# A fused decoder's first stage: batch 1 split at the start, its linear product behind batch 0's, key stores and loads in another order

## The chip, the cores and the metric

The kernel runs on one core of a Trainium2 chip. The core has five engines that run their own instruction streams and wait for each other on semaphores: TensorE (PE), VectorE (DVE), ScalarE (ACT), GpSimd (POOL) and SyncE (SP), which here only waits and issues transfers. Transfers (DMA) run on 16 engines of their own. The metric is the device time of the whole kernel in microseconds, the median of some runs.

## The reference, cut to what matters

A decoder of two layers on `x` (16 batches x 112 tokens x 1024), float32. Each step adds its result to its input and normalises the sum.

```python
x = layernorm(x + x @ (W0 * blockmask).T + bias)            # L0 "attention": a block-masked linear layer
x = layernorm(x + xattn(x, ctx, ctx, mask))                 # 32 heads of 32, 8 shared key/value heads, 375 context rows
x = layernorm(x + gated_slot_ffn(x))                        # routing to 8 of 256 slots, a learned gate
x = layernorm(x + L1_attention(x))                          # causal, over the batch
x = layernorm(x + xattn(x, ctx, ctx, mask))
x = layernorm(x + routed_low_rank_ffn(x))
```

The first line and the cross attention of the first layer are what the change touches. `blockmask` switches 32 x 32 blocks of the 1024 x 1024 weight off; the kernel itself sums the mask over the blocks, masks the weights and splits them.

## The kernel before, in words

The program has three stages: `token_stage` for layer 0 (lines, cross attention and slot layer, batch by batch), `self_attention`, and `token_stage` for layer 1. A float32 product is made of three products of rounded parts (`split_passes`): high by high, high by low, low by high. So each operand is first copied to a high part (`x_hi`, by ScalarE) and the rest is taken as the low part (`x_lo`, by GpSimd or VectorE).

In `token_stage` every engine runs the same loop over turns t (`turns`), from t = -3 in layer 0. In turn t the attention of batch t is computed in 32 steps n (one head each: score, masked minimum, exponential, transposition, weighted values), and beside it the linear layer of batch t + 2, the queries of batch t + 1 and the end of batches t - 1 and t - 2. `on(lag)` says whether batch t + lag exists. The order on each engine is exactly the order in which the code issues; nothing moves it later. The work of an engine waits where it stands, and all that is behind it on the engine waits too.

The lead-in (turns -3 to -1 of layer 0):
- SyncE loads `xt` (the transposed x of batch 0), eight chunks of the block mask and eight of the weights through six buffers (`load_weights`), the bias, `xb` (x of batch 0 by rows), `xt` of batch 1, `craw` (transposed context) and, when the weights are done, the raw weights of the slot layer (`load_update`).
- VectorE reduces the mask chunks (L1064), masks the weights (L1079) and takes their low parts (L1072), then negates the attention mask `nmask` (L1084).
- TensorE makes batch 0's linear product while the weights come (`first_linear`), VectorE adds it to `xb` and normalises it (`linear`, L455) to `xnew`; TensorE transposes `xnew` to queries (L464), ScalarE and VectorE take the parts (`qT_hi`, `qT_lo`).
- Batch 1 follows in turn -1: `xt` split at the end of turn -2 (L771, L438), 48 products (L473), the addition and the normalisation.
- The query parts and the parts of the context (`c_hi`, `c_lo`, scaled) are stored to HBM (`query_parts`, `ctx_parts`) and read back in the layout of the heads: `krep` and `qrep`, halves 0 and 1, four loads each (L256, L273). A score (L482) needs its half of both (semaphore `ld_kq`).

The steps the prediction speaks of are L771 (`x_hi`), L438 (`x_lo`), L762 (`qT_hi`), L1051 (`qT_lo`), L749 (`probs`, the exponential) and L482 (scores). ScalarE's wait for `xt` reads:

```python
if first and on(3) and n == 25:
    if on(2):
        act.wait_ge(lin_ok, 2 * (t + 3))
    act.wait_ge(ld_xt, w.next(ld_xt, 16))
    nc.scalar.copy(x_hi[:], xt[:]).then_inc(x_hi_ok, 1)
```

## Time and profile before

| | us |
|---|---|
| median of 3 runs | 3253.34 (3253.17 to 3255.41) |
| the profiled execution | 3256.68 |
| its span, first to last instruction | 3254.9 |

The page's first two sections: busy time and share of each engine, and the span in 40 slices of 81 us, each digit a busy share in tenths. PEclk is the granted clock of TensorE in tenths of full speed.

```profile
span 3254.9 us, 67042 instructions
...
PE 3086.3 (95%) x25912; PEld 2573.2 (79%) x25912; DVE 1804.2 (55%) x4632; ACT 1340.0 (41%) x3692; POOL 872.4 (27%) x751
...
PE   5999999986899999999999999999999699999997
PEld 3888888874788888888878888888887588888886
DVE  6788888885434432444253323333243488888885
ACT  2777877783211111111111111111111487877773
POOL 2222222212423432243225332443233001111110
PEclk8999999996899999999999999999999799999998
DMA  9777787763112311231144111221124555556651
```

TensorE is busy for 95% of the span. The first slice holds the lead-in, with TensorE at 5 tenths.

### The profile page before, as it was taken

To read this page: it belongs to the slowest core of one execution; us is meant where nothing else is said; L and a number is where in the kernel's file an instruction comes from. 1 tells how busy PE (TensorE), PEld (TensorE's weight loads), DVE (VectorE), ACT (ScalarE), POOL (GpSimd) and SP (SyncE) were. 2 spreads that over 40 slices of the span, in tenths; PEclk is the share of its full clock that TensorE was granted. 3 is DMA by queue.
4 is the path that set the end of the run, shared out by engine and by line. 5 is a ranking of instruction groups with operands and counts; after the bars stand their busy time and mean duration, and the time that the engine had idled before them with its cause. 6 is when DMAs were issued, how large, how long until landed. Compare 5 with 4: busy or idle time off the path is not lost. (4 is left out here: it accounts for less than half of the span.)

```text
span 3254.9 us, 67042 instructions
## 1 busy us (share of the span) xinstructions
PE 3086.3 (95%) x25912; PEld 2573.2 (79%) x25912; DVE 1804.2 (55%) x4632; ACT 1340.0 (41%) x3692; POOL 872.4 (27%) x751
## 2 busy tenths in 40 slices
PE   5999999986899999999999999999999699999997
PEld 3888888874788888888878888888887588888886
DVE  6788888885434432444253323333243488888885
ACT  2777877783211111111111111111111487877773
POOL 2222222212423432243225332443233001111110
PEclk8999999996899999999999999999999799999998
DMA  9777787763112311231144111221124555556651
GB/s 279 191 188 190 191 202 189 183 149 99 53 58 79 91 53 58 72 91 59 51 164 143 53 59 61 83 79 52 52 72 162 157 146 152 153 151 153 152 147 36
DMA packets 226622, 386.73 MB, mean 119 GB/s; under 512 B 55953, under 2 KB 177137, under 8 KB 225794
## 3 DMA queue, kind: packets, MB, share of 16 engines
q1 hardware_dynamic: 222848, 380.25, 42.2%
q8 instruction: 207, 3.39, 0.5%
q10 hardware_dynamic: 3458, 2.20, 0.2%
q14 instruction: 109, 0.89, 0.1%
HBM read 291.46 MB, written 90.91 MB: 117 GB/s over the span
## 5 line engine op out<-in xcount | busy, mean ns | idle before, releaser
L749 ACT ACTIVATE L_probs<-L_masked,L_least 112x375 f32<-112x375 f32 x1024 | 627.9, 615 | 79.1 <-DVE L_least L878 74.9
L878 DVE CUSTOM_DVE_ANT_0 L_masked<-L_scores,L_nmask 112x375 f32<-112x375 f32 x1024 | 553.1, 544 | 172.3 <-PE L_scores L482 135.3
L1445 PE MATMUL sa_banks<-both_hi,sa_w_hi 128*128 128x480 f32 (+2 forms) x1536 | 559.7, 364 | 2.0 <-DVE both_lo L1706 2.0
L1445 PE MATMUL sa_banks<-both_lo,sa_w_hi 128*128 128x480 f32 (+2 forms) x1536 | 550.2, 358 | 0.0
L1445 PE MATMUL sa_banks<-both_hi,sa_w_lo 128*128 128x480 f32 (+2 forms) x1536 | 549.5, 358 | 0.0
L487 PEld LDWEIGHTS L_turned<-ident_sb,L_probs 112*125 112x125 f32 x3072 | 456.2, 189 | 106.0 <-issue 48.1
L487 PE MATMUL L_turned<-ident_sb,L_probs 112*125 112x112 f32 x3072 | 525.2, 280 | 6.5 <-ACT L_probsT L744 3.3
L482 PE MATMUL L_scores<-L_krep,L_qrep 128*112 128x376 f32 x1024 | 417.2, 408 | 8.1 <-DMA L_qrep<-query_parts 6.2
L744 ACT COPY L_probsT<-L_turned 125x336 f32<-125x336 f32 x768 | 337.4, 439 | 175.2 <-PE L_turned L487 168.1
L1747 DVE TENSOR_TENSOR sa_acc<-sa_acc,sa_banks 128x512 f32<-128x512 f32 x224 | 154.1, 688 | 416.5 <-PE sa_banks L1504 416.5
L1504 PE MATMUL sa_banks<-sa_p_hi,sa_o_hi 128*128 128x512 f32 x896 | 365.2, 408 | 0.0
L1504 PE MATMUL sa_banks<-sa_p_lo,sa_o_hi 128*128 128x512 f32 x896 | 355.1, 396 | 0.0
L1504 PE MATMUL sa_banks<-sa_p_hi,sa_o_lo 128*128 128x512 f32 x896 | 355.0, 396 | 0.0
L1445 PEld LDWEIGHTS sa_banks<-both_hi,sa_w_hi 128*128 128x128 f32 x1536 | 288.9, 188 | 34.5 <-issue 6.8
L1713 DVE SCALAR_TENSOR_TENSOR sa_sm<-sa_banks,sa_causal 128x224 f32<-128x224 f32 x64 | 25.1, 392 | 511.2 <-PE sa_banks L1466 511.2
L1445 PEld LDWEIGHTS sa_banks<-both_hi,sa_w_lo 128*128 128x128 f32 x1536 | 288.7, 188 | 23.3
L1445 PEld LDWEIGHTS sa_banks<-both_lo,sa_w_hi 128*128 128x128 f32 x1536 | 289.1, 188 | 21.6
L1614 ACT CAST sa_o_hi<-sa_banks 128x512 fp32r<-128x512 f32 x112 | 66.0, 589 | 508.0 <-PE sa_banks L1487 506.4
L384 POOL TENSOR_TENSOR L_attn<-L_attn,L_xcur 112x512 f32<-112x512 f32 x64 | 82.5, 1288 | 584.2 <-DVEq L891 584.2
L1388 POOL TENSOR_TENSOR sa_w_lo<-sa_raw,sa_w_hi 128x1024 fp32r<-128x1024 f32 x96 | 229.9, 2394 | 14.5 <-issue 1.6
L1386 POOL CAST sa_p_hi<-sa_raw 128x1024 fp32r<-128x1024 f32 x64 | 66.5, 1039 | 564.3 <-PE sa_banks L1504 554.5
L1504 PEld LDWEIGHTS sa_banks<-sa_p_hi,sa_o_hi 128*128 128x128 f32 x896 | 169.0, 189 | 47.9 <-issue 0.4
(289 smaller groups left out, 5054.2 us busy)
## 6 DMA issues: line engine op xcount, KB each, us to landing
L_qrep<-query_parts SPq DMA_DIRECT2D x256, 224.0 KB, 6.2
sa_raw<-in_wqkvU_dram SPq DMA_DIRECT2D x96, 512.0 KB, 3.5
L_krep<-ctx_parts SPq DMA_DIRECT2D x256, 188.0 KB, 4.3
sa_raw<-in_wprojU_dram SPq DMA_DIRECT2D x64, 512.0 KB, 3.5
query_parts<-L_qT_hi SPq DMA_DIRECT2D x64, 224.0 KB, 8.3
query_parts<-L_qT_lo SPq DMA_DIRECT2D x64, 224.0 KB, 9.4
L_xcur<-x SPq DMA_DIRECT2D x32, 448.0 KB, 5.0
L_val<-in_ctx_dram SPq DMA_DIRECT2D x64, 187.5 KB
```

Source lines behind the costliest of these rows:

```text
L384: p.tensor_tensor(attn[0:S, cols], attn[0:S, cols], xcur[0:S, cols], ALU.add).then_inc(sum_ok, 1)
L482: pe.matmul(scores[0:S, (NH * t + n) % 3, 0:TP], qrep[:, gq, r, gi, :], krep[:, 4 * gq + gi, :], start=True, stop=True).then_inc(score_ok, 1)
L487: mm = pe.transpose(turned[0:TC, m % 2, S * j:S * j + S], probs[0:S, m % 4, TC * j:TC * j + TC], ident[0:S, 0:S])
L744: nc.scalar.copy(probsT[:, m % 8, :, :], turned[0:TC, m % 2, 0:TJ * S].rearrange("p (j s) -> p j s", s=S)).then_inc(copied_s, 1)
L749: nc.scalar.activation(probs[0:S, e % 4, :], masked[0:S, e % 4, :], ACT.Exp, bias=least[0:S, e:e + 1], scale=-1.0, accum_out=rsum[0:S, e:e ...
L878: v.tensor_tensor_reduce(out=masked[0:S, n % 4, :], in0=scores[0:S, (NH * t + n) % 3, 0:T], in1=nmask[0:S, :], scale=1.0, scalar=HUGE, op0 ...
L1386: nc.gpsimd.tensor_copy(hi, src)
L1388: done = nc.gpsimd.tensor_tensor(lo, src, hi.bitcast(F32), ALU.subtract)
L1445: mm = pe.matmul(feat[u % 2][i][:, 0:t.stop - t.start], a[:, u % 2, k, :], b[:, k, t], start=(n == 0), stop=(n == 3 * KT - 1))
L1504: mm = pe.matmul(out, a[:, j, c % 2, :], b[:, j, 512 * h:512 * h + 512], start=(i == 0), stop=(i == 3 * QPG - 1))
L1614: nc.scalar.copy(o_hi[:, :, c % 2, :].rearrange("p j (b t) -> p j b t", b=4), mixed).then_inc(o_hi_ok, 1)
L1747: v.tensor_tensor(acc[:, c, cols], acc[:, c, cols], ring[:, b, :], ALU.add).then_inc(ring_free[b], 1)
```

## The change

All of it is in the lead-in of the first stage; line numbers of the changed kernel are about 28 to 46 higher.

- `xT[1]` is loaded at the very beginning, in front of `xT[0]`, into `oT`, and split in turn -3 into `tT_hi` and `tT_lo` (buffers that are free until turn 1). The linear product of batch 1 reads these.
- The first 16 of the 24 products of batch 1's first half stand right behind batch 0's product on TensorE (`HEADSTART`), behind VectorE's reading of the bank.
- `nmask` is negated as VectorE's first work, and waits for the small loads. The bias addition of batch 0 waits until the weights are done (`chunk_done`).
- The parts of batch 0's context are taken in turn -2 and stored (`store_keys`) behind `load_update`. In turn -1 SyncE waits for `x_free`, loads `xb`, stores the queries of batch 0, then `x1`, and loads `krep` half 0, `qrep` half 0, `krep` half 1, `qrep` half 1, both halves of `val`, `craw` of batch 1 and `xt` of batch 2, in this order.
- ScalarE's high part of batch 2's `xt` stands at step 8 of turn -1.

ScalarE before, from its last work on the weights to the first exponentials of turn 0. `L_ra` is a table load, `L_c_hi` the context's high part:

```order
L820 DMA L_ra<-in_valuesT_dram 128x256 x2
L771 CAST L_x_hi<-L_xt 128x896 [waits L0_ld_xt,L0_lin_ok]
L762 CAST L_qT_hi<-L_wide 128x448 [waits L0_turn] x2
L766 ACTIVATE L_c_hi<-L_craw 128x2x375 [waits L0_ld_c]
L771 CAST L_x_hi<-L_xt 128x896 [waits L0_ld_xt,L0_lin_ok]
L762 CAST L_qT_hi<-L_wide 128x448 [waits L0_qT_free,L0_turn]
L749 ACTIVATE L_probs,L_rsum<-L_masked,L_least 112x375 [waits L0_least] x3
L762 CAST L_qT_hi<-L_wide 128x448 [waits L0_turn]
L749 ACTIVATE L_probs,L_rsum<-L_masked,L_least 112x375 [waits L0_least]
L766 ACTIVATE L_c_hi<-L_craw 128x2x375 [waits L0_ld_c]
```

And in the changed kernel, the same stretch:

```order
L861 DMA L_ra<-in_valuesT_dram 128x256 x2
L803 ACTIVATE L_c_hi<-L_craw 128x2x375 [waits L0_ld_c]
L799 CAST L_qT_hi<-L_wide 128x448 [waits L0_turn] x2
L810 CAST L_x_hi<-L_xt 128x896 [waits L0_ld_xt,L0_lin_ok]
L799 CAST L_qT_hi<-L_wide 128x448 [waits L0_qT_free,L0_turn]
L786 ACTIVATE L_probs,L_rsum<-L_masked,L_least 112x375 [waits L0_least] x3
L799 CAST L_qT_hi<-L_wide 128x448 [waits L0_turn]
L786 ACTIVATE L_probs,L_rsum<-L_masked,L_least 112x375 [waits L0_least]
L803 ACTIVATE L_c_hi<-L_craw 128x2x375 [waits L0_ld_c]
```

The context's part has moved ahead of the queries, the split of `xt` for batch 1 is gone from here (it is done at the start), and the split for batch 2 (L810) stands where the one of L771 stood, in front of batch 1's query part and the exponentials.

SyncE before, from the load of `xb` for batch 1 (L298) to half 0 of `krep` for batch 0:

```order
L298 DMA L_xb<-in_x_dram 112x1024
L302 DMA L_xt<-in_xT_dram 128x896 [waits L0_xt_free]
L266 DMA query_parts<-L_qT_hi 128x448 [waits L0_q_lo]
L266 DMA query_parts<-L_qT_lo 128x448
L266 DMA query_parts<-L_qT_hi 128x448 [waits L0_q_lo]
L266 DMA query_parts<-L_qT_lo 128x448
L321 DMA ctx_parts<-L_c_hi 128x376 [waits L0_c_lo_ok]
L321 DMA ctx_parts<-L_c_hi 128x376
L321 DMA ctx_parts<-L_c_lo 128x376 x2
L323 DMA L_craw<-in_ctxT_dram 128x750
L256 DMA L_krep<-ctx_parts 32x4x376 [waits L0_c_stored]
L256 DMA L_krep<-ctx_parts 32x4x376 x3
```

In the changed kernel, from the queries' last stores to `xt` of batch 2:

```order
L266 DMA query_parts<-L_qT_hi 128x448 [waits L0_q_lo]
L266 DMA query_parts<-L_qT_lo 128x448
L330 DMA x<-L_xnew 112x1024
L256 DMA L_krep<-ctx_parts 32x4x376 [waits L0_c_stored]
L256 DMA L_krep<-ctx_parts 32x4x376 x3
L273 DMA L_qrep<-query_parts 32x4x448 [waits L0_q_stored]
L273 DMA L_qrep<-query_parts 32x4x448 x3
L256 DMA L_krep<-ctx_parts 32x4x376 x4
L273 DMA L_qrep<-query_parts 32x4x448 x4
L260 DMA L_val<-in_ctx_dram 125x3x128 x2
L372 DMA L_craw<-in_ctxT_dram 128x750
L374 DMA L_xt<-in_xT_dram 128x896 [waits L0_xt_free]
```

The load of `xt` for batch 2 stood in front of the query stores; it now stands behind all loads of batch 0's keys, queries and values. The key stores (L280) are ahead of this piece.

The diff:

```diff
@@ -273,6 +273,12 @@
 
+            def store_keys(w, nb):
+                sp.wait_ge(c_lo_ok, w.next(c_lo_ok))
+                for part, src in ((0, c_hi), (1, c_lo)):
+                    for h in range(2):
+                        sp.dma_start(ks[nb, part, h], src[:, h, :].bitcast(F32)).then_inc(c_stored, 16)
+
@@ -287,6 +293,7 @@
                 sp.wait_ge(chunk_done, 2 * KT)
+                sp.wait_ge(split_x, 2)
@@ -294,10 +301,14 @@
                     load_weights()
+                if first and t == -1:
+                    sp.wait_ge(x_free, w.next(x_free))
...
                     sp.dma_start(xb[0:S, :], io["x"][t + 2]).then_inc(ld_x, 16)
-                if first and on(3):
-                    if on(2):
+                if first and on(3) and t not in (-2, -1):
+                    if t == -3:
+                        sp.dma_start(oT[:], io["xT"][1]).then_inc(ld_xt, 16)
+                    else:
@@ -307,22 +318,25 @@
                         sp.wait_ge(k_free[1], w.next(k_free[1]))
-                    if first or t:
+                    if t:
                         load_keys(t, 1)
-                    load_queries(t, 1)
+                    if not first or t:
+                        load_queries(t, 1)
...
                     store_queries(w, t + 1, 1)
-                if first and on(1):
-                    sp.wait_ge(c_lo_ok, w.next(c_lo_ok))
-                    for part, src in ((0, c_hi), (1, c_lo)):
-                        for h in range(2):
-                            sp.dma_start(ks[t + 1, part, h], src[:, h, :].bitcast(F32)).then_inc(c_stored, 16)
-                if first and on(2):
+                if first and t == -1:
+                    sp.dma_start(io["x1"][0], xnew[0:S, :]).then_inc(x1_stored, 16)
+                    sp.wait_ge(c_stored, w.next(c_stored, 64))
+                    load_keys(0, 0)
+                if first and on(1) and t >= 0:
+                    store_keys(w, t + 1)
+                if first and on(2) and t != -1:
...
                     load_update()
+                    store_keys(w, 0)
@@ -330,7 +344,7 @@
                         sp.wait_ge(v_free[1], w.next(v_free[1]))
-                    if first or t:
+                    if t:
@@ -340,30 +354,40 @@
                 if on(1):
-                    if first:
+                    if first and t >= 0:
...
                         sp.wait_ge(k_free[0], w.next(k_free[0]))
-                    if first or t >= 0:
+                    if t >= 0:
...
                     load_queries(t + 1, 0)
-                    if not first and t == -1:
+                    if t == -1:
                         load_keys(0, 1)
+                    if first and t == -1:
+                        load_queries(0, 1)
+                        load_values(0, 0)
+                        load_values(0, 1)
+                        sp.dma_start(craw[:], io["ctxT"][1]).then_inc(ld_c, 16)
+                        sp.wait_ge(xt_free, w.next(xt_free))
+                        sp.dma_start(xt[:], io["xT"][2]).then_inc(ld_xt, 16)
...
                     sp.dma_start(io["rows"][t - 2][:, D:D + BOT + 2], z_row[0:S, :]).then_inc(z_stored, 16)
-                if first and on(2):
+                if first and on(2) and t > -2:
...
                         sp.wait_ge(v_free[0], w.next(v_free[0]))
-                    load_values(t + 1, 0 if first or t >= 0 else 1)
+                    if t >= 0:
+                        load_values(t + 1, 0)
+                    elif not first:
+                        load_values(0, 1)
@@ -413,6 +437,7 @@
                         pool.wait_ge(ld_bias, 16)
+                        pool.wait_ge(chunk_done, 2 * KT)
@@ -431,12 +456,15 @@
                     residual(w, 0)
-                if first and on(3):
+                if first and on(3) and t != -2:
...
                     pool.drain().then_inc(xt_free, 1)
+                    if t == -3:
+                        pool.wait_ge(x_hi_ok, w.next(x_hi_ok))
+                        p.tensor_tensor(tT_lo[:], oT[:], tT_hi[:].bitcast(F32), ALU.subtract).then_inc(split_x, 1)
@@ -580,25 +608,34 @@
 
+            HEADSTART = 16
+
...
                     pe.wait_ge(lin_read, w.next(lin_read))
+                left = (tT_hi, tT_lo) if t == -1 else (x_hi, x_lo)
...
                         first_linear(w)
+                        pe.wait_ge(split_x, w.next(split_x))
+                        pe.wait_ge(lin_read, 1)
+                        products(spare[0:S, :], (tT_hi, tT_lo), (w0_hi, w0_lo), slice(0, 512), KT, 0, HEADSTART)
...
                         pe.wait_ge(ra_ok, t - 1)
-                    pe.wait_ge(split_x, w.next(split_x))
+                    if t >= 0:
+                        pe.wait_ge(split_x, w.next(split_x))
...
                     i, j = dealt(LIN[h], n)
+                    if t == -1 and h == 0:
+                        i = max(i, HEADSTART)
                     if i < j:
-                        mm = products(bank[0:S, :], (x_hi, x_lo), (w0_hi, w0_lo), slice(512 * h, 512 * h + 512), KT, i, j)
+                        mm = products(bank[0:S, :], left, (w0_hi, w0_lo), slice(512 * h, 512 * h + 512), KT, i, j)
@@ -761,14 +798,18 @@
                                        wide[:, 0, 0:4 * S].rearrange("p (k s) -> p k s", s=S)).then_inc(q_hi_ok, 1)
-                if first and on(1) and n == 4:
+                if first and ((t, n) == (-2, 24) or on(1) and t >= 0 and n == 4):
...
                     nc.scalar.mul(c_hi[:, :, 0:T], craw[:], -float(HD) ** -0.5).then_inc(c_hi_ok, 1)
-                if first and on(3) and n == 25:
-                    if on(2):
+                if first and on(3) and t != -2 and n == (8 if t == -1 else 25):
+                    if t >= 0:
                         act.wait_ge(lin_ok, 2 * (t + 3))
-                    act.wait_ge(ld_xt, w.next(ld_xt, 16))
+                    if t == -1:
+                        act.wait_ge(lin_ok, 2)
+                    act.wait_ge(ld_xt, w.next(ld_xt, 32 if t == -3 else 16))
                     nc.scalar.copy(x_hi[:], xt[:]).then_inc(x_hi_ok, 1)
+                    if t == -3:
+                        nc.scalar.copy(tT_hi[:], oT[:]).then_inc(x_hi_ok, 1)
@@ -1044,7 +1085,7 @@
 
-            def queries(w, n, on):
+            def queries(t, w, n, on):
@@ -1053,12 +1094,17 @@
                             dve.sem_inc(x_free, 1)
-                if first and on(1) and n == 7:
-                    dve.wait_ge(c_hi_ok, w.next(c_hi_ok))
-                    v.scalar_tensor_tensor(out=c_lo[:, :, 0:T], in0=craw[:], scalar=-float(HD) ** -0.5,
-                                           in1=c_hi[:, :, 0:T].bitcast(F32), op0=ALU.mult, op1=ALU.subtract).then_inc(c_lo_ok, 1)
+                if first and on(1) and t >= 0 and n == 7:
+                    low_keys(w)
+
+            def low_keys(w):
+                dve.wait_ge(c_hi_ok, w.next(c_hi_ok))
+                v.scalar_tensor_tensor(out=c_lo[:, :, 0:T], in0=craw[:], scalar=-float(HD) ** -0.5,
+                                       in1=c_hi[:, :, 0:T].bitcast(F32), op0=ALU.mult, op1=ALU.subtract).then_inc(c_lo_ok, 1)
             def masked_weights():
+                dve.wait_ge(small_in, 16 * len(small))
+                v.tensor_scalar(nmask[0:S, :], nmask[0:S, :], -1.0, None, ALU.mult)
@@ -1080,8 +1126,6 @@
                 low(KT - 1)
-                dve.wait_ge(small_in, 16 * len(small))
-                v.tensor_scalar(nmask[0:S, :], nmask[0:S, :], -1.0, None, ALU.mult)
@@ -1105,7 +1149,9 @@
                     tokens(t, w, n, on)
-                    queries(w, n, on)
+                    queries(t, w, n, on)
+                    if first and (t, n) == (-2, 26):
+                        low_keys(w)
...
                             linear(w, n, on)
```

## Rows read from the trace of the kernel before

**Rows 1.** Waits of TensorE, 66 to 200 us: us in total, times, longest.
```profile
PE L_scores L482 <- DMA L_qrep<-query_parts: 1.9, 1, 1.9
```

**Rows 2.** Timeline near the first scores: start, length (us), engine line op [idle before <-releaser].
```profile
60.30 0.94 ACT L771 CAST L_x_hi<-L_xt 128x896 fp32r<-128x896 f32 x1 [10.83 <-PE L_wide L473]
...
66.98 1.28 PE L482 MATMUL L_scores<-L_krep,L_qrep 128*112 128x376 f32 x3 [1.85 <-DMA L_qrep<-query_parts]
...
68.15 0.62 DVE L1051 TENSOR_TENSOR L_qT_lo<-L_wide,L_qT_hi 128x448 fp32r<-128x448 f32 x1
...
68.82 1.01 PE L464 MATMUL L_wide<-ident_sb,L_xnew 112*128 112x112 f32 x4 [0.56 <-DVE L_qT_lo L1051]
```

**Rows 3.** Timeline, SyncE's queue, key stores and key loads.
```profile
51.77 1.26 SPq L321 DMA_DIRECT2D ctx_parts<-L_c_lo  x2
...
56.99 1.76 SPq L256 DMA_DIRECT2D L_krep<-ctx_parts  x4
```

**Rows 4.** Windows: busy PE, PEld, DVE, ACT, POOL, PEclk, DMA share, GB/s.
```profile
10.00:12.00 2.00, 0.00 (x0) 0.00 (x0) 1.96 (x2) 0.00 (x0) 0.00 (x0) 1.00 1.02 410
...
62.00:64.00 2.00, 0.00 (x0) 0.00 (x0) 0.94 (x2) 0.00 (x0) 0.79 (x2) 0.96 1.05 217
```

**Rows 5.** Timeline of VectorE, lead-in.
```profile
6.39 1.22 DVE L1064 TENSOR_REDUCE L_brow<-L_attn 128x32 f32<-128x1024 int32 x1 [5.26 <-DMA L_attn<-in_bmaskT_dram]
...
15.97 1.22 DVE L1064 TENSOR_REDUCE L_brow<-L_row 128x32 f32<-128x1024 int32 x1
...
35.04 1.22 DVE L1072 TENSOR_TENSOR L_w_lo<-L_xnew,L_w_hi 128x1024 fp32r<-128x1024 f32 x1
36.23 2.24 DVE L1072 TENSOR_TENSOR L_w_lo<-L_xcur,L_w_hi 128x1024 fp32r<-128x1024 f32 x1
38.40 1.44 DVE L1084 TENSOR_SCALAR L_nmask<-L_nmask 112x375 f32<-112x375 f32 x1
...
43.94 0.81 DVE L455 TENSOR_SCALAR L_xnew<-L_xb,L_mv,L_rstd 112x1024 f32<-112x1024 f32 x1 [1.07 <-POOL L_rstd L379]
```

**Rows 6.** Tile nmask: its load (ns min/median/max, first to last start) and its landing.
```profile
L812 ACTq DMA_DIRECT2D L_nmask<-in_mask_dram x1: 452/452/452, 1.7 to 1.7; - x1
...
DMA to landing us min/median/max: 6.7/6.7/6.7
```

**Rows 7.** Timeline of GpSimd, the bias addition and a low half.
```profile
33.61 6.01 POOL L390 TENSOR_TENSOR L_xb<-L_xb,L_bias 112x512 f32<-112x512 f32 x2 [25.64 <-DMA L_xb<-in_x_dram]
...
51.01 2.54 POOL L390 TENSOR_TENSOR L_xb<-L_xb,L_bias 112x512 f32<-112x512 f32 x2 [4.04 <-DMA L_xb<-in_x_dram]
...
64.15 2.07 POOL L438 TENSOR_TENSOR L_x_lo<-L_xt,L_x_hi 128x896 fp32r<-128x896 f32 x1 [0.99 <-DVE L_xnew L455]
```

**Rows 8.** Timeline, first and last of 48 products; VectorE's normalised rows behind them.
```profile
47.85 0.75 PE L473 MATMUL L_spare<-L_w_hi,L_x_hi 128*112 128x512 f32 x1
...
59.86 0.40 PE L473 MATMUL L_wide<-L_w_hi,L_x_lo 128*112 128x512 f32 x1
...
63.19 0.81 DVE L455 TENSOR_SCALAR L_xnew<-L_xb,L_mv,L_rstd 112x1024 f32<-112x1024 f32 x1 [1.06 <-POOL L_rstd L379]
```

**Rows 9.** DMA issues, 50 to 64 us: count, KB each, us from issue to landing.
```profile
L_qrep<-query_parts SPq DMA_DIRECT2D x4, 224.0 KB, 6.0
L_krep<-ctx_parts SPq DMA_DIRECT2D x4, 188.0 KB, 3.7
x<-L_xnew SPq DMA_DIRECT2D x1, 448.0 KB, 4.2
...
query_parts<-L_qT_lo SPq DMA_DIRECT2D x1, 224.0 KB, 4.7
```

**Rows 10.** DMA issues of the whole page, section 6.
```profile
L_val<-in_ctx_dram SPq DMA_DIRECT2D x64, 187.5 KB
```

**Rows 11.** Timeline of ScalarE, batch 1's query copy.
```profile
65.17 0.53 ACT L762 CAST L_qT_hi<-L_wide 128x448 fp32r<-128x448 f32 x1 [3.93 <-PE L_wide L464]
```

**Rows 12.** DMA issues, 64 to 80 us, the load of xt.
```profile
L_xt<-in_xT_dram SPq DMA_DIRECT2D x1, 448.0 KB, 9.8
```

## The prediction

> **What bounds the kernel now.** Read the windows first, then the waits of TensorE, then the timeline of the first 70 us. After the lead-in TensorE is the bound: from 66 to 200 us its longest wait on anyone is one of 1.9, for a transfer, at the start of that stretch [rows 1]. So whatever moves the moment at which TensorE starts its dense work of turn 0 moves the end of the kernel by the same amount. That moment is the transposition of batch 1's query half at 68.82. It follows VectorE's low half of the queries (68.15), which stands on VectorE behind the first score row, and the first score, at 66.98, waited for the last load of `qrep` [rows 2]. So the loads bound the lead-in: four of `krep` issued from 56.99 [rows 3], and four of `qrep` behind them. While only these are in flight the queue moves 217 GB/s with all DMA engines busy; the 4 KB rows of the start move 410 [rows 4].
>
> Call A the end of the last low half of the weights, 38.47 before [rows 5]; what follows is counted from it.
>
> **Start: one more load, mask first.** `xT[1]`, 448 KB, now goes ahead of the mask chunks: 0.46 MB at 410 GB/s is 1.1 us, so the first chunk could be reduced at 7.5 instead of 6.39. But VectorE now first negates `nmask`, whose load on ScalarE's queue, issued at 1.7, lands 6.7 later, at 8.4 [rows 6]. The negation took 1.44 at 38.40, where GpSimd was busy on the bias [rows 5, 7]; an undisturbed one is bounded from below by the 0.81 of a 1024-wide normalisation [rows 5] times 375/1024, 0.3. GpSimd now runs two low halves of about 2.07 each [rows 7] just there; I take the middle, 0.9. First reduction at 9.3 (8.7 to 9.8). The eight reductions ran from 6.39 to 17.19 [rows 5], a gap behind the first among them; at 1.22 and a hand-over, 1.25 each, they end at 19.3: **2.1 later** (1.5 to 2.7). The weights follow at VectorE's own pace. The last low half took 2.24 beside the bias addition, the one before it 1.22 [rows 5]; the addition now waits for `chunk_done`, that is until after it: **1.0 back**. A is 39.6 (39.0 to 40.2), 1.1 late.
>
> **Between A and the first queries.** The bias addition took 6.01 for both halves beside VectorE's weights and 2.54 undisturbed [rows 7]. It now stands behind A and delays the second half of the sums to about A + 2.8, but the negation's 1.44 is gone. Before, the normalisation began at A + 5.5; I count A + 5.7. The low keys (about 0.9) fit in the 1.07 in which VectorE waited for GpSimd's root [rows 5]. `x_ok` of batch 0: A + 6.5. If that cover is gone it costs at most those 0.9. The 16 products put in front (HEADSTART) run in this gap, where TensorE idled. Of 48 products, 47.85 to 60.26 before [rows 8], 32 are left: about 8 us from A + 9.5, batch 1's normalised rows at A + 17.5 + 4, 61.1 against 64.0 [rows 8]. They are there before the loads below have landed, so this saving alone buys nothing.
>
> **SyncE's queue, step by step.** The four key stores now go from A + 5.6, 2.5 us of issue (two took 1.26 [rows 3]), then `xb` to A + 8.5. Query stores wait for the low halves (A + 8.9, A + 11) and end at A + 11.6; `x1` of batch 0 (448 KB) to A + 12; `krep` half 0, 1.8, to A + 13.8. The query stores land 4.7 after their issue [rows 9], so `qrep` half 0 is issued from A + 15.8 to A + 17.6. Nothing after it waits: `krep` half 1, `qrep` half 1, two `val`, `craw`, then `xt` of batch 2, the twelfth issue behind `qrep` half 0, at about A + 23.0. On the wire `x1` comes first and ends around A + 15.2, by its 4.2 of landing [rows 9]. A pair of `krep` and `qrep` halves is 4 x 188 + 4 x 224 = 1648 KB, 1.69 MB, 7.8 us at 217 GB/s. Half 0 lands at A + 23.0 = 62.6. **The scores could start 4.4 earlier than at 66.98**, and that is what the change buys.
>
> **What is late next.** ScalarE's order in the changed kernel has the high half of batch 2's `xt` (L810) right in front of batch 1's query copy and of the first three exponentials. Before, it stood in the same place, but its `xt` had been issued early and it ran at 60.30 [rows 2], waiting for TensorE only. Now it waits for the last load of the burst. Behind `qrep` half 0 come 1.69 MB more (7.8 us, A + 30.8), then 2 x 187.5 + 375 + 448 = 1198 KB (`craw` is 128 x 750 floats; the others [rows 9, 10]), 1.23 MB, 3.0 us at 410 or 5.7 at 217. Landing at A + 33.8 to A + 36.5, and some 0.4 until the waiting engine sees it; I take A + 35.4 = 75.0. Queued behind the wait on ScalarE are batch 1's first query copy, for which VectorE's low half waits, for which TensorE's transposition waits, and `probs` 0, 1, 2, for which all of turn 0's transpositions wait. The chain after the landing: 0.94 [rows 2], a copy of 0.53 [rows 11], a low half of 0.62 and some 0.2 of hand-over, 2.3 in all; TensorE's transposition starts at 77.3 against 68.82: **+8.5**. GpSimd's low half of `xt` (2.07 [rows 7]) runs beside this and is ready at 78.1, when TensorE is done with four transpositions and a score. If it were not, the products would wait for it by less than 1. What might give some back: the three scores are ready and need not be waited for, at most 0.5. TensorE waited for no transfer but this one up to 200 us [rows 1], so that half 1 is in place early gives nothing.
>
> On the order of the queue: before, `xt` landed 9.8 after its issue, behind all that had been issued ahead of it [rows 12]. The page "DMA: Bandwidth & Descriptors" of the Trainium skill, section on queues, rings and completion order, says that an engine consumes a queue's descriptors in ring order while completions may overtake; with the former, `xt` comes last, as counted; were it only the latter that counts, rival 3 would hold.
>
> The profiled execution took 3256.68 around a span of 3254.9, 3.3 above the median of 3253.34. 3256.68 + 8.5 would be 3265.2; put on the median of the runs, **3261.8 us**.
>
> **Rivals.**
> 1. *The queue drains fast.* If the burst from `x1` on (448 + 2 x 1648 + 1198 = 4942 KB, 5.06 MB) moved at the 410 of the start, it would take 12.3 us and `xt` would be bound by its issue: A + 23.0 + 4.2 = 66.8, TensorE at 69.1, **+0.3, 3253.6**. For it: 410 was reached with 4 KB rows. Against it: `krep` and `qrep` are three quarters of the bytes, and alone in flight they had 217 at full share [rows 4]. The section "Anatomy of one DMA" of that page of the Trainium skill gives a transfer a fixed 2.0 us plus its bytes over 436 GB/s; an estimate by it is 13.6 us for the burst. By that rule, the trace disagrees for these loads, with 217.
> 2. *`xt` lands as late after its issue as it did before,* 9.8 [rows 12]: A + 32.8 = 72.4, TensorE at 74.7, **+5.9, 3259.2**. For it: that load also had other loads ahead of it. Against: fewer bytes were ahead.
> 3. *Faster.* ScalarE's wait is no wait, because `xt`'s 16 engines take it past the narrow transfers and it lands by 62.6 less 0.9, A + 22. Then the scores' landing decides, 62.6 against 66.98: **-4.4, 3248.9**. It decides only if `xt` lands before its own counted issue at A + 23, so SyncE would have to be 5 us ahead of my count as well. Against it stands the order of issue.
> 4. *Worse:* SyncE is held up while the queue is full, or the rate of the burst falls under 217 with stores in it: at 180 the 5.06 MB take 28 us from A + 13.7, `xt` at 81.4, TensorE at 83.7, **+14.9, 3268.2**.
>
> **How the numbers follow.** Main case 0.62, with its own range +6 to +10.8 (3259.5 to 3264); rival 1 0.10; rival 2 0.15; rival 3 0.06; rival 4 0.07. A measurement tells a change from none beyond about 0.2%, 6.5 us. Slower by more: 0.57 of the main case, 0.06 of rival 2, all of 4: 0.70. Within: 0.05, 0.09, rival 1 and half of 3: 0.27. Faster by more: 0.03. Range 3253.5 to 3266.5: rival 1's value to the main case's upper end with some of rival 4; outside are rival 3, most of 4 and part of 1.
>
> **What would show it.** Right: ScalarE idle for some 20 us before the cast L810 near 75, released by the DMA `L_xt<-in_xT`; first `probs` after 76; first score near 62.6 and TensorE nearly idle to 77; last low half of the weights near 39.6, 1.2 long. Wrong: L810 near 67 or earlier (rivals 1, 3), `krep` and `qrep` moving well above 217 GB/s together, or new DMA waits of TensorE past 80.

## The result and the profile after

| | before | after |
|---|---|---|
| median of the runs made side by side | 3255.38 us (3250.29 to 3257.75, 9 runs) | 3265.54 us (3263.04 to 3273.03, 9 runs) |
| the profiled execution, its span | 3256.68, 3254.9 | 3269.76, 3268.0 |

The ratio after to before is 1.0038, 95% interval 1.0029 to 1.0047: the change costs about 12 us, between 9 and 15, where 8.5 was forecast. On the runs that the forecast was put on (3253.34) that is about 3265.7, against 3261.8 and a range up to 3266.5. Direction and mechanism came as forecast; the size did not. Medians and ratios here and below are of undisturbed executions; two of the twelve of experiment 4, at 5503 and 5926 us, are left out.

The totals of the page hardly move: TensorE is as busy as before, in a span 13.1 longer.

```profile
PE 3087.6 (94%) x25912; PEld 2573.7 (79%) x25912; DVE 1807.6 (55%) x4632; ACT 1339.8 (41%) x3692; POOL 870.4 (27%) x751
```

**Where the time went.** The waits of TensorE up to 210 us (us in total, times, longest) name the place. The wait for the low half of the queries is 15.3 long; from 66 to 200 us before, nothing was longer than 1.9 [rows 1]. (`[rows n]` are the numbered rows shown ahead of the prediction.)

```profile
PE L_wide L492 <- DVE L_qT_lo L1092: 16.5, 2, 15.3
...
PE L_scores L510 <- DMA L_qrep<-query_parts: 2.5, 1, 2.5
```

The timelines of ScalarE and TensorE show the chain, in the same order as [rows 2]: ScalarE stands idle for 29.49 us, released by the load of `xt`; its cast, its query copy and then its exponentials follow at once, and TensorE gets its transposition at 80.14 against 68.82, 11.3 later.

```profile
78.06 0.94 ACT L810 CAST L_x_hi<-L_xt 128x896 fp32r<-128x896 f32 x1 [29.49 <-DMA L_xt<-in_xT_dram]
78.90 0.53 ACT L799 CAST L_qT_hi<-L_wide 128x448 fp32r<-128x448 f32 x1
79.32 0.61 ACT L786 ACTIVATE L_probs<-L_masked,L_least 112x375 f32<-112x375 f32 x1
```

```profile
63.60 1.28 PE L510 MATMUL L_scores<-L_krep,L_qrep 128*112 128x376 f32 x3 [2.45 <-DMA L_qrep<-query_parts]
80.14 1.01 PE L492 MATMUL L_wide<-ident_sb,L_xnew 112*128 112x112 f32 x4 [15.26 <-DVE L_qT_lo L1092]
...
120.30 0.41 PE L510 MATMUL L_scores<-L_krep,L_qrep 128*112 128x376 f32 x1
```

The last row is the first score of turn 1. Before it began at 109.68:

```profile
109.68 0.41 PE L482 MATMUL L_scores<-L_krep,L_qrep 128*112 128x376 f32 x1
```

So the loss stands at 10.6 there. It is 10.6 in turn 2 (151.08 to 161.72) and in turn 4 (237.93 to 248.56) as well. The last score of layer 0 comes 11.3 late (747.3 to 758.6), the first product of `self_attention` 13.1 (834.7 to 847.8), and the last score of layer 1 still 13.1 (3207.0 to 3220.1). So 10.6 are made in the lead-in. The last 1.8 of the profile arise between the layers, where TensorE has gaps and its granted clock is mostly 0.50 in both kernels; what makes them is not shown.

**The clock behind the hole.** In the changed kernel TensorE is nearly idle from 60 to 80 us and is granted 0.50, the lower of its two levels (1.2 of 2.4 GHz). It works at that level until 83.7, 3.6 behind the late transposition. Before, it also stood at 0.50 around the first scores, and until 74.0, 5.2 behind the transposition.

```profile
60.00:80.00 20.00, 2.26 (x7) 1.42 (x7) 1.11 (x4) 1.95 (x4) 0.93 (x1) 0.50 0.87 212
80.00:83.50 3.50, 3.36 (x12) 2.75 (x13) 1.67 (x7) 2.67 (x9) 3.31 (x3) 0.50 0.35 72
```

Products of 512 columns follow each other by 0.43 at that level and by 0.23 at the full one, so 1.7 less at 0.50 give back 0.8 by an estimate: about the 0.7 between 11.3 and 10.6. The clock came back 3.0 to 5.9 behind that transposition in the kernels below, so the start of turn 1 carries 1 us or more of this, and each kernel has one profile only. The transposition is given too where it matters.

**SyncE's queue** is where the forecast and the trace part.

```profile
50.16 2.29 SPq L330 DMA_DIRECT2D x<-L_xnew  x1
52.49 2.42 SPq L256 DMA_DIRECT2D L_krep<-ctx_parts  x4
55.04 1.77 SPq L273 DMA_DIRECT2D L_qrep<-query_parts  x4
56.85 1.86 SPq L256 DMA_DIRECT2D L_krep<-ctx_parts  x4
58.75 2.13 SPq L273 DMA_DIRECT2D L_qrep<-query_parts  x4
60.92 3.95 SPq L260 DMA_DIRECT2D L_val<-in_ctx_dram  x2
64.91 6.18 SPq L372 DMA_DIRECT2D L_craw<-in_ctxT_dram  x1
71.13 0.43 SPq L374 DMA_DIRECT2D L_xt<-in_xT_dram  x1
```

An issue takes about 0.45. Here two issues of `val` take 3.95 (0.41 and 3.49) and one of `craw` 6.18, so that `xt` is issued at 71.13, not at 62.6. The windows (busy times, then granted clock, DMA share, GB/s) show both what was forecast and what was not: 215 to 228 GB/s from 58 to 68 us, while `krep` and `qrep` are under way, against 217 in [rows 4], and then a hole, 180 and 112, at a DMA share that falls to 0.50.

```profile
62.00:64.00 2.00, 0.40 (x1) 0.41 (x2) 0.00 (x0) 0.00 (x0) 0.00 (x0) 0.50 1.08 223
...
68.00:70.00 2.00, 0.00 (x0) 0.00 (x0) 0.00 (x0) 0.00 (x0) 0.00 (x0) 0.50 0.90 180
70.00:72.00 2.00, 0.00 (x0) 0.00 (x0) 0.00 (x0) 0.00 (x0) 0.00 (x0) 0.50 0.50 112
72.00:74.00 2.00, 0.00 (x0) 0.00 (x0) 0.00 (x0) 0.00 (x0) 0.00 (x0) 0.50 1.00 257
```

### The profile page after: what moved, and what is told of

Its sections match the earlier page's. It is cut to its first block and busy times, and to the rows that moved or that the text cites. A ratio compares the mean times of both kernels' runs of the same rounds, so it can differ in the third digit from the quotient of the medians.

```text
span 3268.0 us, 67041 instructions
## 1 busy us (share of the span) xinstructions
PE 3087.6 (94%) x25912; PEld 2573.7 (79%) x25912; DVE 1807.6 (55%) x4632; ACT 1339.8 (41%) x3692; POOL 870.4 (27%) x751
```

## The experiments

Each kernel was timed beside the kernel before. "Turn 1" is the start of its first score by the profile; the whole time can differ from it by what happens later (13.1 against 10.6 in the profile above). Of a difference in medians, about 3 us to each side are uncertain, by the intervals.

| kernel | median us | ratio, 95% interval | turn 1 | against before |
|---|---|---|---|---|
| before | 3255.38, 3254.13, 3254.83, 3254.09 beside the four groups | | 109.68 | |
| after | 3265.54 | 1.0038, 1.0029 to 1.0047 | 120.30 | +10.6 |
| `xt` two turns early | 3259.53 | 1.0016, 1.0008 to 1.0025 | 114.67 | +5.0 |
| `xt` and `craw` early | 3252.00 | 0.9993, 0.9985 to 1.0002 | 105.75 | -3.9 |
| before, with `xt` late | 3260.68 | 1.0022, 1.0013 to 1.0030 | 118.62 | +8.9 |
| `xt` ahead of `val` | 3260.42 | 1.0021, 1.0012 to 1.0030 | 116.94 | +7.3 |
| `val` out of the burst | 3259.90 | 1.0018, 1.0009 to 1.0026 | 115.51 | +5.8 |
| `xt`, `craw` early, `val` out | 3251.63 | 0.9993, 0.9984 to 1.0001 | 107.26 | -2.4 |
| the same, `x1` store in front | 3255.42 | 1.0002, 0.9993 to 1.0010 | 109.44 | -0.2 |
| `xt`, `craw` early, no products in front | 3252.52 | 0.9997, 0.9989 to 1.0006 | 109.34 | -0.3 |
| `val` cut into 112 and 13 rows | 3258.63 | 1.0013, 1.0004 to 1.0022 | 118.32 | +8.6 |

### 1. `xt` of batch 2 loaded two turns early

```
+                if first and t == -2:
+                    sp.wait_ge(xt_free, w.next(xt_free))
+                    sp.dma_start(xt[:], io["xT"][2]).then_inc(ld_xt, 16)
...
-                        sp.wait_ge(xt_free, w.next(xt_free))
-                        sp.dma_start(xt[:], io["xT"][2]).then_inc(ld_xt, 16)
```

> The changed kernel with one load moved: xt of batch 2 is loaded in turn -2, right behind xb of batch 0, no longer as the last load of the burst. Theory (ScalarE's wait for xt costs all of it): ScalarE's cast of xt runs near 49 instead of 78.06; the first scores land where they did, 63.6, and TensorE's transposition of batch 1 follows 1.8 later, near 65.4, against 80.14 in the changed kernel and 68.82 before. craw of batch 1 is now the last load of the burst and ScalarE needs it behind four exponentials; its issue was held until 71.1, so a second stop of some us until about 73 is expected. Sum: 9 to 14 under the changed kernel, -3 to +3 against the kernel before. Rival 1 (the burst itself is the cost, whichever load ScalarE waits for): +6 or more against before, the stop moved to craw in full. Rival 2 (later stages differ between the programs): still about +12 although the first stage starts early.

The wait for `xt` is gone: TensorE's transposition starts near 65.5, its wait for `qT_lo` is 0.6. But only about half of the loss comes back, where -3 to +3 against before was expected: the expectation priced the second stop too low. The timeline of ScalarE shows what is late next:

```profile
77.00 0.83 ACT L804 ACTIVATE L_c_hi<-L_craw 128x750 fp32r<-128x750 f32 x1 [8.41 <-DMA L_craw<-in_ctxT_dram]
```

and TensorE's waits show who stood behind it, the copy of turned probabilities that ScalarE has to make after `c_hi`:

```profile
PE L_turned L516 <- ACT L_probsT L782: 6.5, 4, 5.3
```

So `craw`, loaded by the same burst, is a second late load with the same mechanism, hidden in the changed kernel by the first.

### 2. `xt` and `craw` both early

```
+                if first and t == -1:
+                    sp.dma_start(craw[:], io["ctxT"][1]).then_inc(ld_c, 16)
+                if first and t == -2:
+                    sp.wait_ge(xt_free, w.next(xt_free))
+                    sp.dma_start(xt[:], io["xT"][2]).then_inc(ld_xt, 16)
...
-                        sp.dma_start(craw[:], io["ctxT"][1]).then_inc(ld_c, 16)
-                        sp.wait_ge(xt_free, w.next(xt_free))
-                        sp.dma_start(xt[:], io["xT"][2]).then_inc(ld_xt, 16)
```

> As the run before, and craw of batch 1 is loaded right behind xb of batch 1 in turn -1, in front of the query stores. Theory: no load of the burst is waited for by ScalarE any more; the scores come about 1 later than 63.6 for the 375 KB in front, TensorE's transposition near 66.4 against 68.82 before: -2.4 against before (-1 to -4), 14 under the changed kernel. Rival 1 (half 1 and val in the burst delay something else, as xb of batch 2): no faster than before, 0 or more. Rival 2 (later stages differ): +10.

The whole loss is gone: from +10.6 to -3.9 at turn 1, and from 1.0038 to 0.9993. The rest of the change (mask first, products in front, earlier key stores and loads) buys 3.9 at turn 1, with a first score at 62.79 against 66.98; the prediction had counted 4.4. In the medians a gain is not resolved, since the interval reaches past 1. SyncE was still held here, 4.28 on the two `val` issues and 5.78 on the store behind them, and no engine on the path waited for what stood behind.

### 3. The kernel before, with its `xt` put behind the loads

```
-                if first and on(3):
+                if first and on(3) and t != -1:
...
-                    if first or t:
+                    if t:
...
-                load_queries(t, 1)
+                if not first or t:
+                    load_queries(t, 1)
...
-                    if not first and t == -1:
+                    if t == -1:
                         load_keys(0, 1)
+                    if first and t == -1:
+                        load_queries(0, 1)
+                        sp.wait_ge(xt_free, w.next(xt_free))
+                        sp.dma_start(xt[:], io["xT"][2]).then_inc(ld_xt, 16)
```

> The kernel before with only this: in turn -1 SyncE loads half 1 of krep and qrep of batch 0 right behind half 0, and xt of batch 2 behind them instead of in front of the query stores. None of the rest of the change is in it. Theory: scores as before at 66.98, half 1 lands about 7.8 later (74.8), xt 1.3 behind it, 76; ScalarE's cast ends at 77, TensorE's transposition at 78.5 to 79.5 against 68.82: +10 (+8 to +12) against before, by one wait alone. Rival (the changed kernel is slow by something else, the early split, the mask first, the head start): within 2 of the kernel before.

This is the mechanism alone, without the rest of the change (the edit also brings half 1 of `krep` and `qrep` forward, to have the burst ahead of `xt`): ScalarE's cast waits 26.62 us for `xt`, and turn 1 is 8.9 late.

```profile
76.38 0.94 ACT L776 CAST L_x_hi<-L_xt 128x896 fp32r<-128x896 f32 x1 [26.62 <-DMA L_xt<-in_xT_dram]
```

Here `xt` was ahead of `val` and was issued in 0.45; the hold of 7.63 fell on `xb`, behind `val`.

### 4. `xt` in front of `val` and `craw`

```
+                        sp.wait_ge(xt_free, w.next(xt_free))
+                        sp.dma_start(xt[:], io["xT"][2]).then_inc(ld_xt, 16)
                         load_values(0, 0)
                         load_values(0, 1)
                         sp.dma_start(craw[:], io["ctxT"][1]).then_inc(ld_c, 16)
-                        sp.wait_ge(xt_free, w.next(xt_free))
-                        sp.dma_start(xt[:], io["xT"][2]).then_inc(ld_xt, 16)
```

> The changed kernel with xt of batch 2 issued in front of the two val loads and craw, right behind half 1 of qrep. In the changed kernel the two val issues took 3.95 and the craw issue 6.18, while the engines' busy share fell to 0.5 at 70 to 72. Theory A (SyncE is held because too many transfers are under way, whatever they are): the xt issue itself is held some us; it lands behind half 1, near 73, at least 4 under 78.06. Theory B (it is held by val's rows of 512 B): the xt issue takes its 0.4 near 61.3 and xt lands 1.3 behind half 1, near 72.5. Both: ScalarE's cast at 72.5 to 74, the kernel 4 to 6 under the changed one, +6 to +8 against before. Rival (bytes alone set the landing): cast at 75.5 to 76, 2 under.

SyncE's queue: `xt` is issued ten microseconds earlier, at 61.23, unheld, so the number of transfers under way (theory A) does not hold it; `val` and `craw` behind it take 12.3 together.

```profile
61.23 0.44 SPq L371 DMA_DIRECT2D L_xt<-in_xT_dram  x1
61.71 7.19 SPq L260 DMA_DIRECT2D L_val<-in_ctx_dram  x2
68.94 5.12 SPq L374 DMA_DIRECT2D L_craw<-in_ctxT_dram  x1
```

Ten microseconds of issue bring only 4.0 at the cast (74.09 against 78.06) and 3.4 at turn 1. `xt` lands 12.8 after its issue: the 3.4 MB of `krep` and `qrep` are ahead of it on the wire, and they move at about 220 GB/s in both kernels. Turn 1 gains less than the cast also because the granted clock came back 4.9 behind the transposition here, 3.6 in the changed kernel.

### 5. `val` out of the burst

Both loads of `val` go behind the loads of turn -2.

```
+                    load_values(0, 0)
+                    load_values(0, 1)
...
-                        load_values(0, 0)
-                        load_values(0, 1)
```

> The changed kernel with both val loads of batch 0 moved out of the burst to turn -2, in front of load_update. craw and xt of batch 2 stay last. Theory V (SyncE was held by val): craw and xt are issued in 0.45 each near 61 to 62; xt lands 2.3 behind half 1 of qrep, near 73.5, ScalarE's cast then, TensorE's transposition near 76: 4 to 5 under the changed kernel, +6 to +7 against before. Theory N (too many transfers under way): craw or xt, the 17th and 18th behind the first krep load, is held for some us as val and craw were, ScalarE's cast at 75 or later. Either way the kernel stays 5 or more above the one before, as ScalarE still waits for the last load.

This tells the two causes of the hold apart. SyncE's queue and ScalarE's cast:

```profile
59.04 1.95 SPq L273 DMA_DIRECT2D L_qrep<-query_parts  x4
61.03 0.48 SPq L372 DMA_DIRECT2D L_craw<-in_ctxT_dram  x1
61.55 0.43 SPq L374 DMA_DIRECT2D L_xt<-in_xT_dram  x1
62.03 0.43 SPq L383 DMA_DIRECT2D x<-L_xnew  x1
```

```profile
73.52 0.94 ACT L810 CAST L_x_hi<-L_xt 128x896 fp32r<-128x896 f32 x1 [23.83 <-DMA L_xt<-in_xT_dram]
```

Behind the same sixteen `krep` and `qrep` loads, four transfers of 375 or 448 KB are issued in 0.43 to 0.48 each. So neither the number of transfers under way nor their bytes hold SyncE; `val` does. Turn 1 is 5.8 late instead of 10.6, and TensorE's transposition starts at 75.60 instead of 80.14. But this edit takes the bytes of `val` (375 KB) from in front of `xt` too, so **the hold and these bytes together cost 4.5 at the transposition and 4.8 at turn 1**; experiment 9 parts them.

The trace of the kernel before already had such a hold, behind its own load of `val`, where it cost nothing that shows:

```profile
81.01 0.39 SPq L260 DMA_DIRECT2D L_val<-in_ctx_dram  x1
81.45 4.06 SPq L338 DMA_DIRECT2D L_xcur<-x  x1
```

### 6. `xt` and `craw` early, and `val` out as well

Edits 2 and 5 together.

> xt and craw early as in e6_xt_craw_early, and the val loads early as well, so that the burst is krep and qrep only. Theory (only what ScalarE waits for costs): like e6, within 1: turn 1 starts near 105.8, -3.9 against the kernel before in the trace, time -2 to -4 against before. Under V SyncE's x1, xb and xt issues behind the burst take below 1 each, under N x1 or xb is still held. Rival: val's rows in front of the key stores delay the first scores by 1 or more and half of the gain goes.

No issue behind the `krep` and `qrep` loads is held any more, yet turn 1 starts 1.5 later than in edit 2 (107.26 against 105.75). Early `val` travels ahead of what is needed first: GpSimd gets batch 1's `xb` 1.9 later (52.29 against 50.40), and the first score, which waits for `qrep`, starts at 64.09, not 62.79. That is the rival in the expectation, not its theory. The medians (3251.63 and 3252.00, from two groups of runs) can't tell these two apart.

### 7. The same, with the store of `x1` at its start

The store now goes ahead of `xb`; all else is as in edit 6.

```
+                    sp.dma_start(io["x1"][0], xnew[0:S, :]).then_inc(x1_stored, 16)
...
-                    sp.dma_start(io["x1"][0], xnew[0:S, :]).then_inc(x1_stored, 16)
```

> As e8, and x1 of batch 0 is stored right behind the wait for x_free, in front of xb and of the query stores, instead of behind them. Its 448 KB then move while the engines have room, and krep's loads are issued at once when the query stores are. Theory (scores wait for qrep's landing): first score at 61.8 to 62.3 against 62.79 in e6; TensorE's transposition of batch 1 (60.5) is just ahead of it; turn 1 starts near 105, -4.7 against before, time -3 to -5. Rival (x1 in front delays the query stores by more than it saves): turn 1 at 106 or later.

It is worse by 2.2 at turn 1, as the rival said, though not by the wait it named. Batch 0's first query stores are issued at 49.48 against 48.17, behind `x1`, `xb` and `craw`, and the `qrep` loads go at 57.81 against 55.62. But the first score, at 66.54, waits for no load; it stands right behind batch 1's transposition at 66.19 (62.69 in edit 6). `xb`, now behind the store, reaches GpSimd at 54.28 against 52.29. TensorE waits 3.68 for VectorE's addition in front of its second half, and then does part of that half at a granted clock of 0.50 (58 to 60 us).

```profile
54.28 2.49 POOL L416 TENSOR_TENSOR L_xb<-L_xb,L_bias 112x512 f32<-112x512 f32 x2 [8.94 <-DMA L_xb<-in_x_dram]
56.32 0.48 PE L503 MATMUL L_wide<-L_w_hi,L_tT_hi 128*112 128x512 f32 x1 [3.68 <-DVE L_xb L1075]
66.19 0.57 PE L494 MATMUL L_wide<-ident_sb,L_xnew 112*128 112x112 f32 x4 [3.90 <-DVE L_xnew L485]
```

### 8. Edit 2 without the sixteen products in front

```
-            HEADSTART = 16
+            HEADSTART = 0
```

> As e6_xt_craw_early, with HEADSTART 0: the 48 products of batch 1 all stand behind the transpositions of batch 0's queries. Theory: x_ok of batch 1 comes some 4 later (TensorE idles 40 to 45 and may be at half clock at 46), its transposition stands in front of the first score, so the first score moves from 62.79 to 65 to 66.5; turn 1 starts at 108 to 109.5, -0.5 to -2 against before; 2 to 4 above e6. Rival (the loads hide it, as in the changed kernel): turn 1 at 105.8 as in e6.

The call, with no product left to make, and its wait for `lin_read` go too. The 3.9 of edit 2 shrink to 0.3 at turn 1 (109.34). Batch 1's query copy on ScalarE starts at 66.89 instead of 61.83 and the first score at 66.63 instead of 62.79, right behind batch 1's transposition at 66.28 (60.81 in edit 2). So by the profiles the 3.9 need both: loads that land earlier, and the products in front, without which batch 1's rows would be what is late; the medians, 3252.52 and 3252.00 with intervals of 3 each way, do not resolve it.

### 9. `val` in two transfers, 112 and 13 rows

```
-                sp.dma_start(val[:, :, P * h:P * h + P],
-                             io["ctx"][nb].rearrange("(j t) c -> t j c", t=TC)[:, :, P * h:P * h + P]).then_inc(ld_v[h], 16)
+                for rows in (slice(0, 112), slice(112, TC)):
+                    sp.dma_start(val[rows, :, P * h:P * h + P],
+                                 io["ctx"][nb].rearrange("(j t) c -> t j c", t=TC)[rows, :, P * h:P * h + P]).then_inc(ld_v[h], 16)
...
-                    pe.wait_ge(ld_v[gq], w.next(ld_v[gq], 16))
+                    pe.wait_ge(ld_v[gq], w.next(ld_v[gq], 32))
```

> The changed kernel, with each load of val cut by rows into two transfers, of 112 and of 13 partitions in place of one of 125; the bytes are the same, and there are two more transfers in the lead-in burst (and one more for each half later). With val out of the burst nothing was held: SyncE issued craw and xt in 0.48 and 0.43 us and the time was 1.0018 of before. Theory P (the hold comes from the 125 partitions, which few DMA engines share, so that their rings fill): the first val issues take under 1 us each, craw after them is not held (under 1 us), xt is issued at 63 to 64, ScalarE's cast of it starts at 75.5 to 77 since val's 0.375 MB still travel ahead of it at 220 to 400 GB/s, the first score of turn 1 starts at 117.5 to 119 (120.30 in the changed kernel), the time is 1.0023 to 1.0033 of before (+7.5 to +10.5). Theory B (what holds is the many small rows of val, 375 of 512 B for each load, whatever engines they lie on, behind 16 transfers under way): the holds stay, 8 to 12 us in all between 60.9 and 72, xt is issued at 70 to 73, the cast starts at 77.5 to 79, the first score of turn 1 at 120 to 122, the time is 1.0035 to 1.0045 of before.

SyncE's queue, with the same bytes of `val` in the burst:

```profile
60.93 1.92 SPq L261 DMA_DIRECT2D L_val<-in_ctx_dram  x4
62.89 0.35 SPq L373 DMA_DIRECT2D L_craw<-in_ctxT_dram  x1
63.29 0.71 SPq L375 DMA_DIRECT2D L_xt<-in_xT_dram  x1
```

The hold is gone: 10.1 us of issue have become 2.3 for more transfers. Of the two theories only P fits. The cast starts at 74.71, 3.4 earlier than in the changed kernel (P: 75.5 to 77, so even P had it late), and TensorE's transposition at 76.79, also 3.4 earlier. Here the bytes of `val` are still ahead of `xt`, so **the hold alone costs 3.4, the bytes of `val` the other 1.2 of experiment 5's 4.5, and the late `xt` without either 6.8**, counted at the transposition (68.82 before). Turn 1, at 118.32 (P: 117.5 to 119), gains only 2.0: the granted clock came back 5.9 behind the transposition, against 3.6 in the changed kernel. The ratio, 1.0013, is below P's 1.0023 to 1.0033, though its interval reaches 1.0022. Why the whole time gained more than turn 1 is open, since later loads of `val` were cut as well, and the one profile does not show the gain behind turn 1.

The DMA share tells more about the hold. The changed kernel while `krep` and `qrep` move, and near the end of its hold:

```profile
66.00:67.00 1.00, 0.00 (x0) 0.00 (x0) 0.00 (x0) 0.00 (x0) 0.00 (x0) 0.50 1.08 226
70.25:71.25 1.00, 0.00 (x0) 0.00 (x0) 0.00 (x0) 0.00 (x0) 0.00 (x0) 0.50 0.36 101
```

Experiment 4, near the end of its hold:

```profile
72.50:74.50 2.00, 0.00 (x0) 0.00 (x0) 0.00 (x0) 0.41 (x1) 0.00 (x0) 0.50 0.36 103
```

This kernel, with `val` cut:

```profile
70.25:71.25 1.00, 0.00 (x0) 0.00 (x0) 0.00 (x0) 0.00 (x0) 0.00 (x0) 0.50 1.19 228
```

With `val` in one piece the share falls from about 1.08 to a floor of 0.36, at 101 to 103 GB/s. It is the same floor in experiments 1 and 2 (0.35 and 0.36), and SyncE's last held issue ends just before the floor does, at 71.09 and 74.06 in the two kernels shown (the floor at 71.5 and 74.5). With `val` cut in two there is no such floor. In experiment 3, with one load of `val` and more queued behind, SyncE was held for 7.63 while the share stayed near 1, so a hold can come without it.

## Why the prediction was right in kind and wrong in size

**Right: what bounds, and which wait replaces which.** ScalarE's cast of batch 2's `xt` took the place of the scores' load. It waits 29.5 for the last load of the burst; behind it come batch 1's query copy, the low half, TensorE's transposition and the exponentials, as counted. Putting the same load late in the kernel before costs 8.9 by itself (experiment 3), taking it away gives 5.6 back at turn 1 (experiment 1). The chain after the cast's start was counted as 2.3 and measured 2.1 (78.06 to 80.14). The 0.4 until the waiting engine sees a landing was put in without a row; in experiments 4, 5 and 9 the cast starts about 0.1 behind the landing of `xt`.

**Right: the rate.** 217 GB/s was taken over from [rows 4], and 215 to 228 were measured from 58 to 68 us. Rival 1, which had the burst at 410, is out. The "Anatomy of one DMA" section of the page "DMA: Bandwidth & Descriptors" of the Trainium skill states its 2.0 us plus bytes over 436 GB/s for transfers that GpSimd issues. The prediction left that out; SyncE issues these, and behind `krep` and `qrep` 448 KB took 12.8 and 11.9 from issue to landing (experiments 4 and 5), where that fit would give an estimate of 3.1.

**The step that failed: the issue of `xt` at A + 23.0.** The prediction gave every load behind `qrep` half 0 its plain issue time. Measured, A is 38.31 and `xt` goes at 71.13, which is A + 32.8. Of the 9.8, the start of the `krep` and `qrep` loads and small drifts make 1.1 (the store of `x1` took 2.29 where about 0.4 was counted), and the two `val` issues and `craw`, 10.13 where 1.4 was counted, make 8.7. The prediction had this as half of rival 4, "SyncE is held up while the queue is full", at a chance of 0.07 and without a price of its own; the rate of 180 that rival 4 was priced with came about only in the hole at the end of the hold.

**Its price is less than its length.** Experiment 9 has the same bytes in the same order, issues `xt` 7.8 earlier (63.29) and starts the cast only 3.4 earlier (74.71 against 78.06), since the wire was busy with `krep` and `qrep` until about 68 anyway. Counted from its own A, 38.87, that cast is at A + 35.8, against A + 35.4 in the forecast, and its transposition at A + 37.9, against A + 37.7. So the forecast's landing was the right one for a queue that is never held.

**A was 1.3 better than forecast.** VectorE ran the mask's negation in 0.77 (counted 0.9), at 8.25, and then the eight reductions at 1.13 each where 1.25 was allowed; before there was a gap behind the first of them [rows 5].

```profile
8.25 0.77 DVE L1107 TENSOR_SCALAR L_nmask<-L_nmask 112x375 f32<-112x375 f32 x1 [7.13 <-DMA L_nmask<-in_mask_dram]
8.95 1.20 DVE L1110 TENSOR_REDUCE L_brow<-L_attn 128x32 f32<-128x1024 int32 x1
...
37.08 1.23 DVE L1118 TENSOR_TENSOR L_w_lo<-L_xcur,L_w_hi 128x1024 fp32r<-128x1024 f32 x1
```

So the errors had opposite signs. The transposition came at A + 41.8 where A + 37.7 was forecast, +4.1, of which the hold is 3.4 by experiment 9 and the rest small drifts; A itself gives -1.3. Together that makes 11.3 of the 8.5. That A came early was luck: with the forecast's A the miss would have been larger. A varies from kernel to kernel by as much as 0.8 (38.31 here, up to 39.11 in the experiments, one profile each).

**The other small steps.** The last low half of the weights shrank from 2.24 to 1.23 once GpSimd's addition came after it, as counted (1.0 back). The low keys (0.89) ended before the root was there and cost nothing. `x_ok` of batch 0 came at A + 7.1, counted A + 6.5; the first score at 63.60, counted 62.6. From A that is 2.3 later than counted, and A being early hides 1.3 of it; the held store of `x1` stands in front of these loads. Batch 1's rows were there before TensorE's transposition at 60.16, counted 61.1. No new DMA wait of TensorE appeared behind 80 us in the first turns.

**One thing the prediction did not name:** `craw` was late too. It was hidden behind `xt` and so did not count for the sum, but anyone who had acted on the forecast by moving `xt` alone would have kept 5.0 of the 10.6. Nor did it name the granted clock: TensorE works at 0.50 for 3.6 behind the late transposition, but before the change it did so for 5.2, so here it took nothing extra.

**What stays open.** The whole time lost 12.4 by the ratio, turn 1 lost 10.6; the interval, 9 to 15, covers both, and where the profile's further 2.5 are made is said above, not why. That the moved loads could be brought to a real gain is not shown: the best kernels here stand at 0.9993 of before, with intervals that reach past 1.

## What to carry to other kernels

A load that is moved behind a burst is late by everything ahead of it on the wire, and it stops whatever stands behind its reader in that engine's order: list those first. Count the issuing engine too: here the issues after `val` (125 partitions) were held for several microseconds, and cutting that transfer to 112 and 13 took the hold away. To price such a hold, keep the bytes and take away only the hold: moving the load out of the way changes both. When one late load is found, look in the same burst for the next one before moving it alone.

## What the runs showed of the hardware that was not expected

An issue on SyncE usually took 0.35 to 0.5 us, but behind sixteen `krep` and `qrep` loads one or two issues were held for 2.7 to 7.6 us each whenever a load of `val` (375 rows of 512 B on 125 partitions) had been put in: 7.63 on `xb`, 2.75 to 6.74 on the second `val` itself, 5.12 to 6.18 on `craw`, 4.41 and 5.78 on a store. Without `val` in the burst no issue behind it was held, and cut as 112 and 13 partitions none took over 0.82. Shorter holds came without a `val` near them, as the 2.29 on `x1`; their cause is not shown.

The page "DMA: Bandwidth & Descriptors" of the Trainium skill says, in the section on why a DMA increments its semaphore by 16, that a transfer is spread over the largest number of engines, at most 16, that divides the slowest dimension of both its sides; by that rule 125 partitions go on 5 engines, 112 on 16 and 13 on 13. The trace agrees: near the end of the hold the DMA share is 0.36 of 16 engines where it is 1.08 with all at work, a third; 5 of 16 is 0.31. And the hold and this floor go with the cut. That the queues of those 5 engines were full, and that this is what holds SyncE, is argued from it and not seen: no view here shows one engine's queue.
